# Where the residual rows, the bf16 cast of h1 and its transposing loads are issued, in a transformer layer on eight cores

## The chip, the cores and the metric

The kernel runs on all 8 cores of one Trainium2 chip. The time is in device microseconds (us), from launch to end, of the slowest of the eight cores; smaller is better. The cores do not talk to each other. Each computes 2,048 rows of the output (half of one of four batch entries) and recomputes the keys and values that it needs.

## The reference, cut to what matters

```python
# x: (4, 4096, 2048) f32; 16 heads of 128; feed-forward width I = 5632
def layer(x):
    q, k, v = heads(tokens(x) @ Wqkv.T)
    ctx = softmax(q @ k.T / sqrt(128)) @ v
    h1 = layernorm(x + ctx @ Wproj.T + bproj)
    w_gu, w_down = dequant_fp4(gate_up), dequant_fp4(down)
    gate, up = split(h1 @ w_gu.T)
    y = (silu(gate) * up) @ w_down.T
    y = y / sqrt(mean(y * y) + 1e-6)
    return layernorm(h1 + y)
```

## The kernel before, in words

Each engine has its own program, written by hand, and runs it in order; engines meet at counting semaphores. TensorE first projects keys, values and queries for the first pair of heads. Then come eight slots of attention (SLOTS), each of 128 steps (STEPS). A step is a score block, its exponential on ScalarE (`act_exp`, tiles P, three buffers), and the context matmuls. While ScalarE works, TensorE fills in matmuls of the next slot's projections. In the last slot the filling is the output projection: 16 tiles of 128 rows (TILES), each of four groups of 512 columns, 16 matmuls a group, in two PSUM banks in turn. It starts at step 60 of the last slot (OC_FIRST), so that part of it runs beside the attention's last exponentials and the rest, about eleven tiles, runs alone. This rest is called the tail below.

For one tile t of the output projection the engines work like this:

- SyncE loads the context transposed (`sp_ctx_load`, a ring of four) and the residual rows of x (`sp_xr_load`, two buffers xr). The load for tile t+2 waits until VectorE has read all of tile t (oc_evac).
- GpSimd adds the bias to the residual rows (`pool_bias`, L918).
- VectorE adds the rows to the PSUM bank group by group (L674) and takes statistics (L677, L681).
- GpSimd forms the reciprocal deviation (`pool_rstd_b`, L928 and L931), and VectorE writes the normalized tile h1f, two buffers (L687).
- GpSimd stores h1f, then does `pool_bias` for tile t+2, and only then `pool_rstd_b` for tile t+1. Its loop is this:

```python
    for tile in range(TILES):
        pool_rstd_b(g, S, M, tile)
        g.wait_ge(S.h1_done, tile + 1)
        g.dma_start(out=M.d_h1[...], in_=M.h1f[tile % 2][:])
        if tile + 2 < TILES:
            pool_bias(g, S, M, tile + 2)
```

- ScalarE casts h1f to bf16 in another order of columns (`act_h1_cast`, L505) and stores it (L509). Casts of tiles 0 to 3 stand between exponentials, at steps fixed in `act_program`; tiles 4 to 15 come after the last exponential.
- VectorE starts on the next tile only when its biased rows are there (xrb_done) and h1f of the tile before is written.

The feed-forward part follows, in four chunks of 512 rows (FCH). A chunk has 44 gate/up operations of 32 matmuls each (`pe_gate_up`, L389 and L393) and then the down projection (`pe_down`, L412). The gate/up weights are in a ring of four buffers of 1 MB (`sp_wgu_load`, L1126); SyncE issues the load for operation n+4 when operation n is done. The rows of h1 come in by transposing loads from the bf16 copy in DRAM (`sp_h1t_load`, L1118), one for each 128 rows, four for a chunk, into one of two buffers. The loads for the next chunk stand on SyncE's queue at operation 10, all four in a row.

Of the kernel before, what the change touches and what calls it, by code (L numbers as in the profile page):

```python
# [24 lines left out]
SLOTS = 8  # L25
STEPS = 128
# [13 lines left out]
TILES = TOK // 128  # L40
OC_FIRST = 60
CTXT_RING = 4
WP_EARLY = (58, 60, 62)

FCH = 4
WGU_RING = 4
WD_RING = 9
PAIR_BANKS = (0, 2, 6, 4)

# [16 lines left out]
def oc_groups_done(i):  # L66

    return max(0, STEP_UNITS * (i + 1 - OC_FIRST) // GROUP_UNITS)
# [43 lines left out]
""".split()  # L112
SEVERAL = {"ctx_stored": 2, "pk_in": 2, "wt_stored": 2, "ctxt_in": CTXT_RING, "xr_in": 2, "h1b_stored": 2, "h1t_in": 2, "wgu_in": WGU_RING, "wd_in": WD_RING, "out_last": 2, "wdx_in": 2}
POOL_ONE = "bias_in wv_in wq_in w1_in".split()
# [21 lines left out]
class Mem:  # L136


    def __init__(self, nc):
# [21 lines left out]
        def at(offset, name, shape, dt):  # L161
            return nc.alloc_sbuf_tensor_at(name, shape, dt, offset=offset)
# [18 lines left out]
        self.hffnT = at(r1, "hffnT", [128, GU_OPS, 512], BF16)  # L181
        self.wd = [at(r1 + 45056 + 4096 * j, f"wd{j}", [128, 4, 512], BF16) for j in range(WD_RING)]

# [10 lines left out]
        self.y = [at(r2 + 8192 * j, f"y{j}", [128, H], F32) for j in range(4)]  # L194
        self.wgu = [at(r3 + 8192 * j, f"wgu{j}", [128, 4, 4, 256], BF16) for j in range(WGU_RING)]

# [172 lines left out]
def pe_gate_up(t, S, M, ch, op, exact):  # L369
    kc = ch * GU_OPS + op  # L370
    b = PAIR_BANKS[kc % 4]
    t.wait_ge(S.wgu_in[kc % WGU_RING], 16 * (kc // WGU_RING + 1))
    if op == 0:
# [9 lines left out]
    elif op == 3:  # L383
        t.wait_ge(S.ctx_evac, SLOTS * QBLOCKS)
        if not exact:
            t.wait_ge(S.flag_done, 1)
    w = M.wgu[kc % WGU_RING]
    for kt in range(HC):
# [9 lines left out]
def pe_down(t, S, M, ch, oc):  # L398
    for ut in range(DN_UT):
        du = (ch * 4 + oc) * DN_UT + ut  # L400
        t.wait_ge(S.wd_in[du % WD_RING], 16 * (du // WD_RING + 1))
        if oc == 0:
# [7 lines left out]
        for tt in range(4):  # L410
            for j in range(4):
                mm = t.matmul(M.bank((oc % 2) * 4 + tt),  # L412
                              M.hffnT[:, 4 * ut + j, tt * 128:(tt + 1) * 128],
                              M.wd[du % WD_RING][:, j, :],
                              start=(ut == 0 and j == 0), stop=(ut == DN_UT - 1 and j == 3))
# [4 lines left out]
def pe_down_last(t, S, M):  # L420
# [3 lines left out]
    for tt in range(4):  # L424
        for ut in range(DN_UT):
            du = first + ut
            if tt == 0 and ut < WD_RING:
                t.wait_ge(S.wd_in[du % WD_RING], 16 * (du // WD_RING + 1))
            elif tt == 0:
# [67 lines left out]
                 scale=NORM).then_inc(S.exp_done, 1)  # L497


def act_h1_cast(a, S, M, tile):  # L500

    a.wait_ge(S.h1_done, tile + 1)
    if tile >= 2:
        a.wait_ge(S.h1b_stored[tile % 2], 16 * (tile // 2))
    a.copy(out=M.h1b[tile % 2][:].rearrange("t (u j p) -> t u j p", u=4, j=4),  # L505
           in_=M.h1f[tile % 2][:].rearrange("t (u p j) -> t u j p", u=4, j=4)
           ).then_inc(S.h1b_done, 1)
    a.wait_ge(S.h1b_done, tile + 1)
    a.dma_start(out=M.d_h1b[tile * 128:(tile + 1) * 128, :],  # L509
                in_=M.h1b[tile % 2][:]).then_inc(S.h1b_stored[tile % 2], 16)  # L510


def act_silu(a, S, M, kc):
# [30 lines left out]
def act_program(a, S, M, exact):  # L544
    a.wait_ge(S.consts, 1)
    g = 0
    while g < GROUPS:
        act_proj_evac(a, S, M, g)
        g += 1
    tile = 0  # L550
    for n in range(SLOTS * STEPS):
        act_exp(a, S, M, n)
        last = n % STEPS == STEPS - 1
        while g < groups_done(n if exact and last else n - 1):
            act_proj_evac(a, S, M, g)
            g += 1
        if n >= (SLOTS - 1) * STEPS and 4 * (tile + 1) <= oc_groups_done(n % STEPS - 5):
            act_h1_cast(a, S, M, tile)
            tile += 1
    while tile < TILES:  # L560
        act_h1_cast(a, S, M, tile)
        tile += 1

    for ch in range(FCH):
        for op in range(GU_OPS):
            act_silu(a, S, M, ch * GU_OPS + op)
        for oc in range(4 if ch + 1 < FCH else 3):
            act_y_evac(a, S, M, ch, oc)
    for tt in range(4):
        act_last_norm(a, S, M, tt)  # L570
    r = TILES - 1
    a.wait_ge(S.l_norm, 12)
    a.wait_ge(S.l_done, 4)
    a.dma_start(out=M.d_out[r * 128:(r + 1) * 128, 1024:2048],
                in_=M.res[3][:, 1024:2048]).then_inc(S.out_last[1], 16)
# [525 lines left out]
                          ).then_inc(S.ctxt_in[tile % CTXT_RING], 16)  # L1101


def sp_xr_load(y, S, M, tile):
    if tile >= 2:
        y.wait_ge(S.oc_evac, 4 * (tile - 1))
    y.dma_start(out=M.xr[tile % 2][:],
                in_=M.d_xrows[tile * 128:(tile + 1) * 128, :]).then_inc(S.xr_in[tile % 2], 16)


def sp_h1t_load(y, S, M, ch, tiles):
    if ch >= 2:
        y.wait_ge(S.up_done, GU_OPS * (ch - 1))
    for j in range(2):
        y.wait_ge(S.h1b_stored[j], 32 if ch == 0 else 16 * (TILES // 2))
    for tt in tiles:
        tile = 4 * ch + tt
        y.dma_start_transpose(out=M.h1T[ch % 2][:, tt, :, :],  # L1118
                              in_=M.d_h1b[tile * 128:(tile + 1) * 128, :]
                              ).then_inc(S.h1t_in[ch % 2], 16)  # L1120


def sp_wgu_load(y, S, M, kc):
    if kc >= WGU_RING:
        y.wait_ge(S.up_done, kc - WGU_RING + 1)
    y.dma_start(out=M.wgu[kc % WGU_RING][:].rearrange("p j u o -> p (j u o)"),  # L1126
# [13 lines left out]
def sp_program(y, S, M, exact):  # L1140
    if not exact:
        y.wait_ge(S.proj_done, group_offset(7))
        sp_codes(y, S, M, 0)
        sp_codes(y, S, M, 1)
    for c in range(SLOTS * QBLOCKS - QBLOCKS):
        if exact and c % QBLOCKS == 0:
            sp_row_max(y, S, M, c // QBLOCKS)
        sp_ctx_store(y, S, M, c)
        for u in () if exact else dequant_units(c):
            sp_weights(y, S, M, u)  # L1150
    if exact:
        sp_row_max(y, S, M, SLOTS - 1)
    y.wait_ge(S.pv_done, (SLOTS - 1) * STEPS)
    sp_xr_load(y, S, M, 0)
    sp_xr_load(y, S, M, 1)
    xr = ctxt = 0
    for i in range(STEPS):
        if i % 16 == 15:
            sp_ctx_store(y, S, M, (SLOTS - 1) * QBLOCKS + i // 16)
        if i == 34:  # L1160
            y.wait_ge(S.proj_done, SLOTS * GROUPS)
            while ctxt < CTXT_RING:
                sp_ctx_load(y, S, M, ctxt)
                ctxt += 1
        if 4 * (xr + 1) <= oc_groups_done(i - 2):
            sp_xr_load(y, S, M, xr + 2)
            xr += 1
        while ctxt - CTXT_RING < xr and 32 * (ctxt // 4 + 1) <= i:
            sp_ctx_load(y, S, M, ctxt)
            ctxt += 1  # L1170
    y.wait_ge(S.pv_done, SLOTS * STEPS)
    for j in range(2):
        y.wait_ge(S.ctx_stored[j], 16 * (SLOTS * QBLOCKS // 2))
    while xr + 2 < TILES:
        if xr == TILES - 5:
            sp_wgu_load(y, S, M, 0)
            sp_wgu_load(y, S, M, 1)
        if xr >= TILES - 4:
            sp_h1t_load(y, S, M, 0, range(2 * (xr - TILES + 4), 2 * (xr - TILES + 4) + 2))
        while ctxt < TILES and ctxt - CTXT_RING <= xr:  # L1180
            sp_ctx_load(y, S, M, ctxt)
            ctxt += 1
        sp_xr_load(y, S, M, xr + 2)
        xr += 1
    sp_wgu_load(y, S, M, 2)
    sp_wgu_load(y, S, M, 3)
    for ch in range(FCH):
        for op in range(GU_OPS):
            kc = ch * GU_OPS + op + WGU_RING
            if kc < FCH * GU_OPS:  # L1190
                sp_wgu_load(y, S, M, kc)
            if op == 10 and ch + 1 < FCH:
                sp_h1t_load(y, S, M, ch + 1, range(4))
            if op == 34 and ch == 0:
                for du in range(WD_RING):
                    sp_wd_load(y, S, M, du)
            if op == 34 and ch == FCH - 1:
                y.wait_ge(S.up_done, (FCH - 1) * GU_OPS)
                for j in range(2):
                    y.dma_start(out=M.wdx[j][:],  # L1200
                                in_=M.d_wdn[3, WD_RING + j]).then_inc(S.wdx_in[j], 16)
        for k in range(4 * DN_UT):
            du = ch * 4 * DN_UT + k + WD_RING
            if du < FCH * 4 * DN_UT - 2:
                sp_wd_load(y, S, M, du)
    for tt in range(4):
        r = 4 * (FCH - 1) + tt
        cols = slice(0, 2048 if tt < 3 else 1024)
        y.wait_ge(S.l_norm, 3 * tt + (3 if tt < 3 else 2))
        if tt < 3:  # L1210
            y.wait_ge(S.l_done, tt + 1)
        y.dma_start(out=M.d_out[r * 128:(r + 1) * 128, cols],
                    in_=M.res[res_slot(r)][:, cols]).then_inc(S.out_last[0], 16)
# [140 lines left out]
```

## Time and profile before

| | us |
|---|---|
| median of 3 runs | 4144.91 (4142.04 to 4147.2) |
| profiled execution | 4153.74 |
| its span on the slowest core, core 2 | 4152.0 |
| spans of the eight cores | 4127.6 to 4152.0 |
| TensorE busy, core 2 | 4060.1 (98%) |
| ScalarE busy, core 2 | 1400.2 (34%) |
| GpSimd busy, core 2 | 286.4 (7%) |

The profile follows one execution. A span goes from a core's first to its last instruction. PE is TensorE, PEld its weight loads, DVE VectorE, ACT ScalarE, POOL GpSimd and SP SyncE; a q behind the name is the engine's issuing of DMAs. L505 is line 505 of the kernel. All times of an instruction are counted from the start of the span.

### The profile page before, as it was taken

Reading aid. Unit: us, or ns where it says so; the run is one execution under the profiler, and the core shown is the slowest. Engines: PE = TensorE matmul, PEld = TensorE weight load, DVE = VectorE, ACT = ScalarE, POOL = GpSimd, SP = SyncE. Lnnn points to the kernel's source line nnn. Section 1 sums busy time; section 2 is a strip of 40 time slices with the busy share of each in tenths; the row PEclk is TensorE's granted clock in tenths of the full one; section 3 lists DMA queues with packets and bytes.
Section 4 is the critical chain, followed back from the end, with each engine's and each line's share of the span. In section 5 each row is a group of like instructions: output and inputs, shape, how many; then the busy total and the mean of one; then the engine's idle time right before and its main releaser. Section 6 shows DMA issues by size and latency. Waiting matters only on the chain.

```text
span 4152.0 us, 66120 instructions; the slowest of 8 cores (4127.6 to 4152.0 us)
## 1 busy us (share of the span) xinstructions
PE 4060.1 (98%) x26491; PEld 2296.5 (55%) x26881; DVE 948.6 (23%) x1433; ACT 1400.2 (34%) x1610; POOL 286.4 (7%) x434
## 2 busy tenths in 40 slices
PE   7999999999999999999999999999999999999998
PEld 4666666666666766666554444444444444444443
DVE  0054452222222223220234100022100300022124
ACT  1355555555555555557642100000000000000001
POOL 1100000000000000000223000000000000000000
PEclk9999999999999999999999999999999999999999
DMA  9777776465655655656459545447444654446433
GB/s 146 130 172 169 178 165 126 107 137 121 124 119 118 140 104 120 135 119 111 110 157 261 191 167 199 159 155 231 152 157 152 201 189 152 157 164 216 162 127 123
DMA packets 251041, 635.65 MB, mean 153 GB/s; under 512 B 115184, under 2 KB 137712, under 8 KB 212720
## 3 DMA queue, kind: packets, MB, share of 16 engines
q1 hardware_dynamic: 202496, 426.29, 31.6%
q0 software_dynamic: 45792, 196.10, 25.5%
q10 hardware_dynamic: 2448, 8.91, 0.5%
q8 instruction: 225, 3.69, 0.4%
q14 instruction: 80, 0.66, 0.0%
HBM read 643.83 MB, written 119.54 MB: 184 GB/s over the span
## 4 chain that ended last, share of the span: by engine, by line
PE 93%; SPq 2%; DMA 2%; issue 1%; ACT 1%; DVE 0%; POOL 0%; ACTq 0%; DVEq 0%; POOLq 0%
PE pJ L283 16%; PE pC L339 11%; PE pJ L269 11%; PE pS L320 10%; PE pS L412 7%; PE pS L393 7%; PE pS L389 7%; PE pC L389 4%; PE pJ L393 3%; PE pC L393 3%; PE pJ L389 3%; PE pJ L361 3%; PE pC L412 3%; PE pJ L412 3%; SPq L1118 2%
## 5 line engine op out<-in xcount | busy, mean ns | idle before, releaser
L496 ACT ACTIVATE P<-pS 128x1024 bf16<-128x1024 f32 x1024 | 1027.8, 1026 | 356.8 <-PE pS L320 342.6
L283 PE MATMUL pJ<-x,wq 128*128 128x512 bf16 x2984 | 756.9, 381 | 28.5 <-DMA x<-xc 23.8
L339 PEld LDWEIGHTS pC<-V,P 128*128 128x128 bf16 x8192 | 549.8, 98 | 168.0 <-issue 11.3
L339 PE MATMUL pC<-V,P 128*128 128x129 bf16 x8192 | 634.0, 220 | 3.6 <-DVE ctxg L613 3.1
L320 PE MATMUL pS<-Q,K 128*128 128x512 bf16 x1829 | 561.7, 379 | 18.9 <-ACT P L496 7.5
L269 PE MATMUL pJ<-wq,x 128*128 128x256 bf16 x4096 | 514.8, 273 | 0.4
L283 PEld LDWEIGHTS pJ<-x,wq 128*128 128x128 bf16 x3072 | 301.0, 98 | 381.9 <-issue 33.4
L269 PEld LDWEIGHTS pJ<-wq,x 128*128 128x128 bf16 x4096 | 400.7, 98 | 134.8
L609 DVE RECIPROCAL rcp<-pC 128x4 f32<-128x4 f32 x64 | 11.7, 183 | 1477.9 <-PE pC L339 1477.9
L393 PE MATMUL pS<-h1T,wgu 128*128 128x512 bf16 x1408 | 318.3, 379 | 0.0
L389 PE MATMUL pS<-h1T,wgu 128*128 128x512 bf16 x1408 | 318.3, 379 | 0.0
L412 PE MATMUL pS<-wd,hffnT 128*128 128x512 bf16 x1380 | 303.1, 379 | 1.5
L905 POOL DMA_DIRECT2D x<-xc x256 | 138.3, 558 | 1743.6 <-PE pJ L283 1089.0
L361 PE MATMUL pJ<-wp,ctxT 128*128 128x512 bf16 x1001 | 232.8, 380 | 9.1 <-DVE r L674 7.8
L517 ACT ACTIVATE sg<-pS 128x512 bf16<-128x512 f32 x88 | 52.4, 597 | 532.5 <-PE pS L389 532.5
L389 PEld LDWEIGHTS pS<-h1T,wgu 128*128 128x128 bf16 x1408 | 137.9, 98 | 166.0
L412 PEld LDWEIGHTS pS<-wd,hffnT 128*128 128x128 bf16 x1408 | 137.8, 98 | 166.1
L393 PEld LDWEIGHTS pS<-h1T,wgu 128*128 128x128 bf16 x1408 | 137.8, 98 | 166.1
L389 PE MATMUL pC<-h1T,wgu 128*128 128x512 bf16 x704 | 163.5, 386 | 13.5 <-DMA wgu<-wgu_scr 13.5
L695 DVE TENSOR_TENSOR hffnT<-sg,pS 128x512 bf16<-128x512 bf16 x88 | 60.6, 688 | 498.6 <-PE pS L393 492.1
L361 PEld LDWEIGHTS pJ<-wp,ctxT 128*128 128x128 bf16 x1024 | 100.0, 98 | 129.7 <-issue 11.4
L320 PEld LDWEIGHTS pS<-Q,K 128*128 128x128 bf16 x2048 | 157.0, 98 | 11.5 <-issue 8.4
(107 smaller groups left out, 2647.8 us busy)
## 6 DMA issues: line engine op xcount, KB each, us to landing
wgu<-wgu_scr SPq DMA_DIRECT2D x176, 1024.0 KB, 4.9
x<-xc POOLq DMA_DIRECT2D x256, 512.0 KB, 12.4
wd<-wdn_scr SPq DMA_DIRECT2D x174, 512.0 KB, 3.5
wgu_scr<-bits SPq DMA_DIRECT2D x44, 1024.0 KB, 5.1
wdn_scr<-bits SPq DMA_DIRECT2D x44, 512.0 KB, 4.6
xr<-xrows SPq DMA_DIRECT2D x16, 1024.0 KB, 7.1
h_scr<-h1f POOLq DMA_DIRECT2D x16, 1024.0 KB, 7.1
res<-h_scr POOLq DMA_DIRECT2D x16, 1024.0 KB, 8.9
```

Of the source, the lines that this page charges most:

```text
L269: mm = t.matmul(out[:, tt * 256:(tt + 1) * 256], x[:, hc, (2 * h + tt) * 128:(2 * h + tt + 1) * 128], M.wq[:, pair, 1, hc, :], start=(hc = ...
L283: mm = t.matmul(out, M.wq[:, pair, part, hc, h * 128:(h + 1) * 128], x[:, hc, :], start=(hc == 0), stop=(hc == HC - 1))
L320: mm = t.matmul(M.pS[n % 2][:, h * 512:(h + 1) * 512], M.K[s % 2][:, l, kt * 128:(kt + 1) * 128], M.Q[s % 2][:, l, qc * 512:(qc + 1) * 512 ...
L339: mm = t.matmul(M.pC[:, o:o + 129], M.P[n % 3][:, h * 512 + qt * 128:h * 512 + (qt + 1) * 128], M.V[s % 2][:, 2 * p + h, l, :], start=(p = ...
L361: mm = t.matmul(M.bank(6 + q % 2), M.ctxT[tile % CTXT_RING][:, hc, :], M.wp[2 * oc + hc // 8][:, hc % 8, :], start=(hc == 0), stop=(hc == ...
L389: mm = t.matmul(M.bank(b), w[:, kt % 4, kt // 4, 0:128], M.h1T[ch % 2][:, :, kt, :], start=(kt == 0), stop=(kt == HC - 1))
L393: mm = t.matmul(M.bank(b + 1), w[:, kt % 4, kt // 4, 128:256], M.h1T[ch % 2][:, :, kt, :], start=(kt == 0), stop=(kt == HC - 1))
L412: mm = t.matmul(M.bank((oc % 2) * 4 + tt), M.hffnT[:, 4 * ut + j, tt * 128:(tt + 1) * 128], M.wd[du % WD_RING][:, j, :], start=(ut == 0 an ...
L496: a.activation(out=M.P[n % 3][:], in_=M.pS[n % 2][:], func=AF.Exp, bias=0.0, scale=NORM).then_inc(S.exp_done, 1)
L695: v.tensor_tensor(out=M.hffnT[:, kc % GU_OPS, :], in0=M.sg[kc % 2][:], in1=M.bank(PAIR_BANKS[kc % 4] + 1), op=ALU.mult).then_inc(S.h_done, 1)
L905: g.dma_start(out=M.x[gc % 2][:, 4 * q:4 * q + 4, :], in_=M.d_x[w, ch, :, 4 * q:4 * q + 4, :]).then_inc(S.x_in[(gc % 2) * 4 + q], 16)
L1118: y.dma_start_transpose(out=M.h1T[ch % 2][:, tt, :, :], in_=M.d_h1b[tile * 128:(tile + 1) * 128, :]).then_inc(S.h1t_in[ch % 2], 16)
```

## The change

Three things are done to the code. First, the cast of a tile is cut into four casts of 512 columns; beside the exponentials one such quarter follows each of four exponentials. Second, the residual rows of tiles 2 to 15 are no longer loaded by SyncE: ScalarE issues the load for tile t+2 behind the store of the bf16 copy of tile t. Third, the transposing loads for the next chunk are issued one at a time, at operations 8, 15, 22 and 29. The transposing loads for the first chunk stay in pairs.

```diff
+H1T_OPS = (8, 15, 22, 29)
-def act_h1_cast(a, S, M, tile):
+def act_h1_cast(a, S, M, k):
+    tile, ut = divmod(k, 4)
+    cols = slice(512 * ut, 512 * (ut + 1))
     a.wait_ge(S.h1_done, tile + 1)
     if tile >= 2:
         a.wait_ge(S.h1b_stored[tile % 2], 16 * (tile // 2))
-    a.copy(out=M.h1b[tile % 2][:].rearrange("t (u j p) -> t u j p", u=4, j=4),
-           in_=M.h1f[tile % 2][:].rearrange("t (u p j) -> t u j p", u=4, j=4)
-           ).then_inc(S.h1b_done, 1)
+    cast = a.copy(out=M.h1b[tile % 2][:, cols].rearrange("t (j p) -> t j p", j=4),
+                  in_=M.h1f[tile % 2][:, cols].rearrange("t (p j) -> t j p", j=4))
+    if ut < 3:
+        return
+    cast.then_inc(S.h1b_done, 1)
     a.wait_ge(S.h1b_done, tile + 1)
     a.dma_start(out=M.d_h1b[tile * 128:(tile + 1) * 128, :],
                 in_=M.h1b[tile % 2][:]).then_inc(S.h1b_stored[tile % 2], 16)
+    if tile + 2 < TILES:
+        a.wait_ge(S.oc_evac, 4 * (tile + 1))
+        a.dma_start(out=M.xr[tile % 2][:], in_=M.d_xrows[(tile + 2) * 128:(tile + 3) * 128, :]
+                    ).then_inc(S.xr_in[tile % 2], 16)
...
-        if n >= (SLOTS - 1) * STEPS and 4 * (tile + 1) <= oc_groups_done(n % STEPS - 5):
-            act_h1_cast(a, S, M, tile)
-            tile += 1
-    while tile < TILES:
-        act_h1_cast(a, S, M, tile)
-        tile += 1
+        if n >= (SLOTS - 1) * STEPS and 4 * (k // 4 + 1) <= oc_groups_done(n % STEPS - 5):
+            act_h1_cast(a, S, M, k)
+            k += 1
+    for k in range(k, 4 * TILES):
+        act_h1_cast(a, S, M, k)
...
-def sp_xr_load(y, S, M, tile):
-    if tile >= 2:
-        y.wait_ge(S.oc_evac, 4 * (tile - 1))
-    y.dma_start(out=M.xr[tile % 2][:],
-                in_=M.d_xrows[tile * 128:(tile + 1) * 128, :]).then_inc(S.xr_in[tile % 2], 16)
...
-        if 4 * (xr + 1) <= oc_groups_done(i - 2):
-            sp_xr_load(y, S, M, xr + 2)
-            xr += 1
+        if 4 * (done + 1) <= oc_groups_done(i - 2):
+            done += 1
...
-    while xr + 2 < TILES:
-        if xr == TILES - 5:
+    for tile in range(done, TILES - 2):
+        if tile == TILES - 5:
             sp_wgu_load(y, S, M, 0)
             sp_wgu_load(y, S, M, 1)
...
-        sp_xr_load(y, S, M, xr + 2)
-        xr += 1
...
-            if op == 10 and ch + 1 < FCH:
-                sp_h1t_load(y, S, M, ch + 1, range(4))
+            if op in H1T_OPS and ch + 1 < FCH:
+                tt = H1T_OPS.index(op)
+                sp_h1t_load(y, S, M, ch + 1, range(tt, tt + 1))
```

## Rows read from the trace of the kernel before

**Rows 1.** Spans and mean granted TensorE clock, two of eight cores.

```profile
core 2: 4152.0 us, clock 0.996
...
core 5: 4136.4 us, clock 0.997
```

**Rows 2.** TensorE's waits, core 2: instruction, releaser, total us, times, longest.

```profile
PE pC L389 <- DMA wgu<-wgu_scr: 13.5, 2, 7.1
PE pJ L361 <- DVE r L674: 7.8, 3, 3.3
```

**Rows 3.** The same waits of core 5.

```profile
PE pJ L361 <- DVE r L674: 3.4, 1, 3.4
...
PE pC L389 <- DMA wgu<-wgu_scr: 2.8, 1, 2.8
```

**Rows 4.** TensorE's waits, core 2, from 2020 to 2140 us.

```profile
PE pS L320 <- ACT P L496: 6.0, 4, 1.9
```

**Rows 5.** Timeline around tile 0's cast, core 2: start, us, engine, operation, [idle before].

```profile
2015.26 1.02 ACT L496 ACTIVATE P<-pS 128x1024 bf16<-128x1024 f32 x1 [0.94 <-PE pS L320]
...
2018.44 0.59 PE L320 MATMUL pS<-Q,K 128*128 128x512 bf16 x2
...
2029.93 3.94 ACT L505 CAST h1b<-h1f 128x2048 bf16<-128x2048 f32 x1
...
2033.95 0.38 ACTq L509 DMA_DIRECT2D h1b_scr<-h1b  x1
...
2035.66 0.59 PE L320 MATMUL pS<-Q,K 128*128 128x512 bf16 x2 [1.34 <-ACT P L496]
```

**Rows 6.** ScalarE's groups by shape, core 2: busy, mean ns | idle before.

```profile
L505 ACT CAST h1b<-h1f 128x2048 bf16<-128x2048 f32 x16 | 62.6, 3915 | 123.0 <-DVE h1f L687 123.0
...
L528 ACT COPY y<-pS 128x512 f32<-128x512 f32 x32 | 18.8, 586 | 298.9 <-PE pS L412 298.9
```

**Rows 7.** Timeline of the tail's end, core 2: tile 15's rows, tile 14's h1f.

```profile
2269.55 0.52 SPq L1107 DMA_DIRECT2D xr<-xrows  x1
...
2279.23 4.50 POOL L918 TENSOR_TENSOR xr<-xr,bias 128x2048 f32<-128x2048 f32 x1 [9.94 <-DMA xr<-xrows]
2283.71 0.22 POOL L928 TENSOR_SCALAR epsB<-aggB 128x1 f32<-128x1 f32 x1
...
2284.75 1.34 DVE L687 TENSOR_SCALAR h1f<-r,aggB,rstdB 128x2048 f32<-128x2048 f32 x1 [5.87 <-POOL rstdB L931]
2286.24 3.85 ACT L505 CAST h1b<-h1f 128x2048 bf16<-128x2048 f32 x1 [14.08 <-DVE h1f L687]
```

**Rows 8.** Timeline, core 2: h1f of tile 4, ahead of the tail.

```profile
2134.09 1.35 DVE L687 TENSOR_SCALAR h1f<-r,aggB,rstdB 128x2048 f32<-128x2048 f32 x1 [1.33 <-POOL rstdB L931]
```

**Rows 9.** Residual-row loads L1107, core 2, from 2150 to 2275 us.

```profile
L1107 SPq DMA_DIRECT2D xr<-xrows x9: 504/525/1951, 2151.7 to 2269.5; - x9
...
DMA to landing us min/median/max: 6.4/7.8/9.7
```

**Rows 10.** The same loads from 2020 to 2140 us.

```profile
L1107 SPq DMA_DIRECT2D xr<-xrows x5: 352/353/357, 2024.7 to 2131.7; - x5
...
DMA to landing us min/median/max: 5.2/5.4/5.4
```

**Rows 11.** Transposing loads L1118, core 2: issue time ns, minimum, median, maximum.

```profile
L1118 SPq DMA_TRANSPOSE h1T<-h1b_scr x16: 2968/4513/9328, 2241.3 to 3311.6; - x16
```

**Rows 12.** The chain that ended last, core 2: start, us, what.

```profile
2850.53 11.26 DMA wgu<-wgu_scr
```

**Rows 13.** Timeline, core 2, around the loads for chunks 2 and 3.

```profile
2827.96 22.47 SPq L1118 DMA_TRANSPOSE h1T<-h1b_scr  x4
...
2862.06 5.93 PE L389 MATMUL pC<-h1T,wgu 128*128 128x512 bf16 x16 [7.07 <-DMA wgu<-wgu_scr]
...
2867.83 3.62 PE L393 MATMUL pC<-h1T,wgu 128*128 128x512 bf16 x16
...
3326.85 5.65 PE L389 MATMUL pC<-h1T,wgu 128*128 128x512 bf16 x16 [6.47 <-DMA wgu<-wgu_scr]
```

More of the change, by code:

```diff
@@ L549, in act_program @@
         g += 1
-    tile = 0
+    k = 0
     for n in range(SLOTS * STEPS):
@@ L1153, in sp_program @@
     y.wait_ge(S.pv_done, (SLOTS - 1) * STEPS)
-    sp_xr_load(y, S, M, 0)
-    sp_xr_load(y, S, M, 1)
-    xr = ctxt = 0
+    for tile in range(2):
+        y.dma_start(out=M.xr[tile][:],
+                    in_=M.d_xrows[tile * 128:(tile + 1) * 128, :]).then_inc(S.xr_in[tile], 16)
+    done = ctxt = 0
     for i in range(STEPS):
@@ L1164, in sp_program @@
                 ctxt += 1
-        if 4 * (xr + 1) <= oc_groups_done(i - 2):
-            sp_xr_load(y, S, M, xr + 2)
-            xr += 1
-        while ctxt - CTXT_RING < xr and 32 * (ctxt // 4 + 1) <= i:
+        if 4 * (done + 1) <= oc_groups_done(i - 2):
+            done += 1
+        while ctxt - CTXT_RING < done and 32 * (ctxt // 4 + 1) <= i:
             sp_ctx_load(y, S, M, ctxt)
@@ L1173, in sp_program @@
         y.wait_ge(S.ctx_stored[j], 16 * (SLOTS * QBLOCKS // 2))
-    while xr + 2 < TILES:
-        if xr == TILES - 5:
+    for tile in range(done, TILES - 2):
+        if tile == TILES - 5:
             sp_wgu_load(y, S, M, 0)
             sp_wgu_load(y, S, M, 1)
-        if xr >= TILES - 4:
-            sp_h1t_load(y, S, M, 0, range(2 * (xr - TILES + 4), 2 * (xr - TILES + 4) + 2))
-        while ctxt < TILES and ctxt - CTXT_RING <= xr:
+        if tile >= TILES - 4:
+            tt = 2 * (tile - TILES + 4)
+            sp_h1t_load(y, S, M, 0, range(tt, tt + 2))
+        while ctxt < TILES and ctxt - CTXT_RING <= tile:
             sp_ctx_load(y, S, M, ctxt)
             ctxt += 1
-        sp_xr_load(y, S, M, xr + 2)
-        xr += 1
     sp_wgu_load(y, S, M, 2)
```

## The prediction

> **What bounds the kernel now.** I read the spans of the cores first: core 2 has 4152.0 us, core 5 has 4136.4, both at a granted clock of nearly 1 [rows 1]. So this is the fast level of 2.4 GHz nearly throughout, and the clock is no cause of the difference. TensorE is busy 98% of the span, so only what makes TensorE wait counts. Its list of waits shows three causes that the change touches. On core 2 they are 13.5 us for gate/up weights, 7.8 us for VectorE's reading of the output projection's banks [rows 2], and 6.0 us, in four waits, for exponentials between 2020 and 2140 us [rows 4]. On core 5 the first two are 2.8 and 3.4 us [rows 3]. A perfect repair of all three would be worth some 27 us on core 2 and 12 on core 5, before what the clock adds.
>
> **The quarter casts.** One cast takes 3.9 us [rows 6]. At tile 0 it follows an exponential, holds the next ones back, and the score matmul waits 1.34 us [rows 5]. Four such casts lie beside exponentials and there are four waits, 6.0 us in all [rows 4]. A copy of 512 columns takes 0.586 us [rows 6] and an exponential of 1024 takes 1.02 [rows 5]. If both cost the same per column, the fixed part of an instruction is 0.15 us (an estimate). A quarter then costs (3.915 - 0.15)/4 + 0.15 = 1.09 us and four cost 4.37. The lower bound is 3.91 in all, with no fixed part; the upper is 4.7, if the fixed part is 0.25. I take 4.37.
>
> Beside the exponentials a step lasts 0.94 + 1.02 = 1.96 us of ScalarE's time [rows 5]. A quarter and an exponential need 2.11, so ScalarE falls behind by 0.15 in each of four steps, and by two DMA issues of 0.38 [rows 5] and 0.35 [rows 10] and some 0.2 of waits. That is about 1.5 us. How much can it fall behind? An exponential ends at 2016.28 and the score matmuls that need its buffer start at 2018.44 [rows 5]: 2.16 us. The quarters fit, and 6.0 us are gained. If they do not fit, the gain is between 0 and 6.
>
> **The residual rows.** This part decides the result. SyncE now issues the load for tile t+2 when VectorE has read tile t. In the changed kernel the load is behind the cast and the store of tile t on ScalarE, and the cast cannot start before h1f of tile t is written. GpSimd, in turn, adds the bias for tile t+2 *before* it computes the reciprocal deviation of tile t+1, without which h1f of tile t+1 cannot be written. The second half of this is visible already: for tile 15 the bias starts at 2279.23, 9.68 us after its load was issued, and the deviation of tile 14 starts at 2283.71, when the bias ends [rows 7]. New is that the load itself waits for h1f. So there is a closed loop with one tile in it, from h1f of tile t to h1f of tile t+1:
>
> - h1f's end to the cast's start, 0.15 (2286.09 to 2286.24) [rows 7]
> - four quarter casts, 4.37
> - the gap to the store, 0.08, and its issue, 0.38 [rows 5], and 0.05 to the next issue (estimated)
> - the landing of 1 MB of rows, L
> - 0.15 from landing to GpSimd's start (estimated)
> - the bias, 4.50, and from the start of L928 to the end of h1f 2284.75 + 1.34 - 2283.71 = 2.38 [rows 7]
>
> The sum is 12.06 + L. For L the tail's nine loads show 6.4 to 9.7 us, median 7.8 [rows 9]; the five beside attention show 5.2 to 5.4 [rows 10]. In the new order the store of the bf16 tile, 512 KB, is just ahead of the load on the same queue, while the slower pace thins the traffic. I take 7.9, near the tail's median, and keep 5.4 and 9.7 as ends. A link of the loop is then 20.0 us, with 17.5 and 21.8 as ends.
>
> Now from h1f of tile 4, which ends at 2135.44 [rows 8], to h1f of tile 14, which ends at 2286.09 [rows 7], there are ten links. They take 150.65 us, 15.1 each, the stalls included. The loop needs more than that even with its shortest landing, so it sets the pace of all ten, up to the load for tile 15. TensorE can't run away, since it has two banks and VectorE reads the next tile only when h1f is written. The first load meets little traffic (6.4), so ten links take 18.5 + 9 x 20.0 = 198.5 us. The tail gets 47.9 us longer. The ends are +24.0 (L = 5.4, ten times 17.46) and +67 (L = 9.7). The tail stalls of 7.8 us lie inside the 150.65 and are not subtracted again. On core 5 the links were shorter by the difference of the waits, 7.8 - 3.4, so it loses 52.3.
>
> Beside the exponentials the same loop costs nothing. Five load issues lie between 2024.7 and 2131.7, 26.8 us apart [rows 10]. Four quarters in four steps take 3 x 1.96 + 1.09 = 7.0 us instead of 4.37, and with L = 5.4 the loop needs about 20 us. Some 6 us of cover remain. SyncE loses the row loads, and its weight and transposing loads come no later.
>
> The Trainium skill speaks against this move (DMA: Bandwidth & Descriptors, "Issuing engines are not separate DMA queues"): DMAs started by ScalarE, SyncE or GpSimd run on the same 16 DMA engines and interleave. By that rule another issuing engine shortens no landing, and no run here yet shows it.
>
> **The transposing loads.** SyncE spends 22.47 us on issuing four [rows 13]. The weight load behind them then needs 11.26 us [rows 12]. TensorE waits 7.07 and, for the next chunk, 6.47 us [rows 13]. After each wait 16 matmuls take 5.93 and 5.65 us where others take 3.62 [rows 13]; the granted clock has fallen for a moment to the lower level, 1.2 GHz, and this adds 2.3 + 2.0. Core 2 has 13.5 + 4.3 = 17.8 us to gain, core 5 has 2.8 + 2.2 = 5.0.
>
> One load at a time occupies SyncE for 4.5 us, 9.3 at most [rows 11]. A weight load is issued three operations before its use, 6 x 3.5 = 21 us. Even the worst pair, 9.3 + 11.26 = 20.6, just fits, and the usual one easily. I take the whole 17.8. The lower bound is nothing, if the single ones stall TensorE as well.
>
> **The sum**, against the profiled execution's 4153.7 us: 4153.7 + 47.9 - 6.0 - 17.8 = 4177.8 for core 2. Core 5 gives 4136.4 + 1.7 around the span + 52.3 - 6.0 - 5.0 = 4179.4. Cores that stalled differently before come out alike, since the same loop paces them. The profiled execution is 8.8 us above the median of the runs, 4144.9, mostly because of core 2's two weight stalls; with these gone I expect no such difference and forecast 4178 for the median, 33 us or 0.8% slower.
>
> **Rivals.**
>
> *The rows land as fast as beside attention.* With L = 5.4 the tail loses only 24.0, and the gains of 23.8 cancel it: 4153.9. For it speaks that the five loads with little traffic took 5.4 [rows 10]; against it, that none of nine in the tail was under 6.4 [rows 9]. With core 5's numbers it is 4155.5, so it ends at the border of no change. Chance 0.08.
> The Trainium skill's fit (DMA: Bandwidth & Descriptors, "Anatomy of one DMA") is 2.0 us + bytes/436 GB/s, an estimate of 4.4 us for 1 MB, which would give a link of 16.5 and about 4144, no change; the trace disagrees, its fastest such load taking 5.2.
>
> *The loop does not close, or is shorter than the tail's present pace: faster.* The row loads would have to leave the path, so that the casts' 6.0 and the weights' 17.8 remain, and also the 7.8 stall goes: core 2 would be at 4122, the slowest core near 4128. The point from which the kernel is faster at all is L = 3.7 us (a link of 15.7). Against it: the code orders cast, store and load on one engine, and no landing is under 5.2. Chance 0.05.
>
> *Single transposing loads still stall TensorE.* One slow issue with a slow landing eats the 21 us of cover. The price is 17.8 at most: 4195. Against it is the first batch of four, for chunk 1, which caused none of the two waits. Chance 0.05.
>
> *The quarters still delay exponentials* as the whole cast does: +6, so 4184. The slack of 2.16 against 1.5 speaks against it. Chance 0.07.
>
> **How the numbers follow.** My forecast has 0.75. The range 4155 to 4195 goes from L = 5.5 to L = 9.5 and takes in both of the last rivals. A measurement of this kernel tells about 0.2% (8.3 us) from no change. Faster: 0.05. Same, which is the first rival's better half: 0.06. Slower: 0.89.
>
> **What would show it.** In the changed profile: a new, large wait of TensorE at L361 for VectorE (r L674), about 5 us in each of ten tiles; h1f (L687) every 20 us in the tail; GpSimd's bias (L918) ending just as L928 starts; quarter casts of 1.1 us; no wait of L320 for exponentials near the casts; no wait of L389 for weights. I am wrong if h1f comes every 14 to 15 us in the tail.

## The result, and the profile after

The changed kernel takes 4181.05 us (median of 4 runs, 4179.87 to 4182.23), the kernel before 4144.91 (median of 3). The ratio is 1.0088, 95% interval 1.0068 to 1.0107: slower by 0.9%, 36 us. The forecast was 4178. Medians and ratios here and below leave out executions in which the clock of a die was disturbed; where only one or two are left, they are given singly. The ratios are the recorded ones and can differ a little from the quotient of the two medians.

The spans of all eight cores are close together now, 4164.8 to 4178.3 where they were 4127.6 to 4152.0, as the forecast had it from one common pace. Two of them, with the mean granted clock:

```profile
core 2: 4164.8 us, clock 0.995
...
core 5: 4178.3 us, clock 0.994
```

TensorE's waits on core 5, the slowest (instruction, releaser, total us, times, longest), answer to [rows 2 to 4]:

```profile
PE pJ L362 <- DVE r L683: 47.3, 10, 21.1
...
PE pS L321 <- ACT P L497: 1.3, 3, 0.9
```

The wait for VectorE at the output projection has gone from 3.4 to 47.3 us on this core and is on every tile of the tail. The waits for gate/up weights are gone from the list, on all eight cores. The waits for exponentials have fallen from 7.0 to 1.3 us.

ScalarE's groups by shape, core 5, against [rows 6]: a quarter takes 1.11 us.

```profile
L509 ACT CAST h1b<-h1f 128x512 bf16<-128x512 f32 x64 | 67.6, 1111 | 171.6 <-DVE h1f L696 171.6
```

One turn of the loop in the timeline of core 5, from h1f of one tile to h1f of the next. It answers to [rows 7].

```profile
2163.95 1.35 DVE L696 TENSOR_SCALAR h1f<-r,aggB,rstdB 128x2048 f32<-128x2048 f32 x1 [6.84 <-POOL rstdB L940]
2165.44 4.14 ACT L509 CAST h1b<-h1f 128x512 bf16<-128x512 f32 x4 [14.06 <-DVE h1f L696]
...
2166.30 15.66 PE L362 MATMUL pJ<-wp,ctxT 128*128 128x512 bf16 x64 [4.26 <-DVE r L683]
...
2169.65 0.34 ACTq L515 DMA_DIRECT2D h1b_scr<-h1b  x1
2170.08 0.40 ACTq L519 DMA_DIRECT2D xr<-xrows  x1
...
2176.68 4.50 POOL L927 TENSOR_TENSOR xr<-xr,bias 128x2048 f32<-128x2048 f32 x1 [10.20 <-DMA xr<-xrows]
2181.16 0.22 POOL L937 TENSOR_SCALAR epsB<-aggB 128x1 f32<-128x1 f32 x1
...
2182.20 1.35 DVE L696 TENSOR_SCALAR h1f<-r,aggB,rstdB 128x2048 f32<-128x2048 f32 x1 [5.18 <-POOL rstdB L940]
```

Read it from above. Everything in it waits for the line before: the casts for h1f, the row load for the casts and the store, the bias for the load (GpSimd idle 10.20 us), the deviation (L937) for the bias, h1f for the deviation. One turn is 2182.20 - 2163.95 = 18.25 us. TensorE works 15.66 us of it, at the lower clock for part of that, and then waits for VectorE. It does not set the pace: the statistics of this tile are ready at 2177.02 us, the bias ends at 2181.18.

There is one turn unlike the others. The same timeline later, tile 11 to tile 12:

```profile
2252.45 19.39 SPq L1120 DMA_TRANSPOSE h1T<-h1b_scr  x4
...
2256.86 1.35 DVE L696 TENSOR_SCALAR h1f<-r,aggB,rstdB 128x2048 f32<-128x2048 f32 x1 [7.15 <-POOL rstdB L940]
...
2262.99 0.47 ACTq L519 DMA_DIRECT2D xr<-xrows  x1
...
2288.08 4.48 POOL L927 TENSOR_TENSOR xr<-xr,bias 128x2048 f32<-128x2048 f32 x1 [28.69 <-DMA xr<-xrows]
...
2293.59 1.35 DVE L696 TENSOR_SCALAR h1f<-r,aggB,rstdB 128x2048 f32<-128x2048 f32 x1 [23.66 <-POOL rstdB L940]
```

This row load, for tile 13, is issued at 2262.99, in the middle of four transposing loads for the first chunk, and needs 25 us to land. The turn takes 36.7 us. SyncE no longer stops for row loads, so the two pairs of transposing loads go out as one group of four. Before, on the same core, the four also followed each other closely, but the row load for tile 13 stood ahead of them on SyncE's own queue and that for tile 14 between the pairs:

```profile
2238.61 0.51 SPq L1107 DMA_DIRECT2D xr<-xrows  x1
2239.28 12.52 SPq L1118 DMA_TRANSPOSE h1T<-h1b_scr  x2
2251.92 0.49 SPq L1107 DMA_DIRECT2D xr<-xrows  x1
2252.57 17.11 SPq L1118 DMA_TRANSPOSE h1T<-h1b_scr  x2
```

No row load of that tail took more than 9.0 us to land. So no gap between the transposing loads was lost. What changed is where the row load starts: no longer in line with them on SyncE's queue but on another, in the middle of the group. All ten row loads of the tail on this core (start and issue time of the instruction in ns; landing in us), against [rows 9], which are of core 2:

```profile
L519 ACTq DMA_DIRECT2D xr<-xrows x10: 395/396/468, 2133.3 to 2317.2; - x10
...
DMA to landing us min/median/max: 5.6/6.4/24.9
```

Every core has such a turn, between the casts of tiles 11 and 12: 22.4 us on core 2, 24.7 on core 0, 30.2 on core 6.

### The profile page after: what moved, and what is told of

Same layout as the page of the kernel before. It is cut to its first block, busy times and chain, and to the rows that moved or that the text cites. A ratio compares the mean times of both kernels' runs of the same rounds, so it can differ in the third digit from the quotient of the medians.

```text
span 4178.3 us, 66672 instructions; the slowest of 8 cores (4164.8 to 4178.3 us)
## 1 busy us (share of the span) xinstructions
PE 4087.4 (98%) x26881; PEld 2297.5 (55%) x26881; DVE 947.9 (23%) x1433; ACT 1404.7 (34%) x1658; POOL 286.1 (7%) x434
## 4 chain that ended last, share of the span: by engine, by line
PE 92%; DMA 3%; issue 1%; ACT 1%; POOL 1%; DVE 1%; ACTq 0%; POOLq 0%; DVEq 0%
PE pJ L284 15%; PE pC L340 11%; PE pJ L270 10%; PE pS L321 10%; PE pS L394 7%; PE pS L413 7%; PE pS L390 7%; PE pJ L390 4%; PE pC L394 4%; PE pC L390 4%; PE pJ L394 4%; PE pJ L413 3%; PE pC L413 3%; DMA xr<-xrows 2%; PE pJ L362 2%
## 5 line engine op out<-in xcount | busy, mean ns | idle before, releaser
L321 PE MATMUL pS<-Q,K 128*128 128x512 bf16 x2048 | 609.0, 379 | 1.3 <-ACT P L497 1.3
L390 PE MATMUL pS<-h1T,wgu 128*128 128x512 bf16 x1408 | 318.2, 379 | 0.0
L362 PE MATMUL pJ<-wp,ctxT 128*128 128x512 bf16 x1024 | 245.9, 393 | 47.3 <-DVE r L683 47.3
L390 PEld LDWEIGHTS pS<-h1T,wgu 128*128 128x128 bf16 x1408 | 137.8, 98 | 166.2
L390 PE MATMUL pJ<-h1T,wgu 128*128 128x512 bf16 x704 | 159.1, 379 | 0.0
```

The lines of the kernel that those rows point to most:

```text
L321: mm = t.matmul(M.pS[n % 2][:, h * 512:(h + 1) * 512], M.K[s % 2][:, l, kt * 128:(kt + 1) * 128], M.Q[s % 2][:, l, qc * 512:(qc + 1) * 512 ...
L362: mm = t.matmul(M.bank(6 + q % 2), M.ctxT[tile % CTXT_RING][:, hc, :], M.wp[2 * oc + hc // 8][:, hc % 8, :], start=(hc == 0), stop=(hc == ...
L390: mm = t.matmul(M.bank(b), w[:, kt % 4, kt // 4, 0:128], M.h1T[ch % 2][:, :, kt, :], start=(kt == 0), stop=(kt == HC - 1))
```

## The experiments

Each was profiled and timed beside the kernel before; "before" after a time is the kernel before on the same chip. The line numbers move a little from kernel to kernel.

### Rows back on SyncE, the rest as changed

```diff
 (changed kernel)
-    if tile + 2 < TILES:                       # ScalarE, end of act_h1_cast
-        a.wait_ge(S.oc_evac, 4 * (tile + 1))
-        a.dma_start(out=M.xr[tile % 2][:], ...)
...
+            sp_xr_load(y, S, M, done + 2)       # SyncE, beside attention
...
+        sp_xr_load(y, S, M, tile + 2)           # SyncE, tail, behind sp_ctx_load
```

> The changed kernel with the residual-row loads back on SyncE, where the kernel before has them; quarter casts and single transposing loads stay. Theory (the rows' place behind the cast closes the loop and costs all of the loss): the links between casts in the tail go from 18.3 back to about 15 us, and the gains of the other two parts stay, 6 us of casts and on the slowest core some 10 us of weight waits: about 4130 us (4124 to 4138), ratio to before about 0.996. Rival (the quarter casts or the single transposing loads carry part of the loss): above 4146.

Measured: 4131.7 us (median of 4), before 4151.1; ratio 0.9957 (0.9937 to 0.9976). In the profiled execution all cores lie between 4121.0 and 4129.8. The waits of its slowest core, core 5:

```profile
PE pJ L362 <- DVE r L679: 4.0, 1, 4.0
...
PE pS L321 <- ACT P L497: 1.1, 2, 0.9
```

On this core the ten links from tile 4's cast to tile 14's take 147.1 us, 14.7 each, where the changed kernel's core 5 needs 201.7. One part, the place of the row loads, carries the whole loss, about 50 us between this kernel and the changed one. The rival is out. The other two parts together make the kernel 0.4% faster.

### Only the rows moved

```diff
 (kernel before; act_h1_cast(tile) with the whole cast)
     a.dma_start(out=M.d_h1b[...], in_=M.h1b[tile % 2][:])...
+    if tile + 2 < TILES:
+        a.wait_ge(S.oc_evac, 4 * (tile + 1))
+        a.dma_start(out=M.xr[tile % 2][:], ...)
...
 (SyncE)
-        sp_xr_load(y, S, M, xr + 2)
```

> The kernel before with only the residual rows moved to ScalarE, behind the store of the whole cast; whole casts and four transposing loads in a row as before. Theory: the links are 0.25 us shorter than in the changed kernel, since a whole cast takes 3.9 and not 4.2 us, so about 18.0; the 6 us of exponentials' waits and the weight waits of 3 to 13 us are back: about 4190 us (4183 to 4200). Rival (the cuts into quarters make the chain long): near 4150.

Measured: 4197.8 and 4209.2 us, before 4151.1. The loop needs no quarters to close. The times are 8 and 19 us over the 4190 that was expected. A part of that is in TensorE's waits for exponentials, 8.9 to 10.1 us on the eight cores, where the kernel before has 6.9 to 7.5; the rest I did not trace. On the slowest core, core 7, row loads land in 5.7 to 12.8 us, median 7.2:

```profile
L516 ACTq DMA_DIRECT2D xr<-xrows x10: 396/624/1558, 2147.5 to 2321.1; - x10
...
DMA to landing us min/median/max: 5.7/7.2/12.8
```

### The bias behind the deviation

```diff
 (changed kernel, GpSimd)
     for tile in range(TILES):
         pool_rstd_b(g, S, M, tile)
+        if 1 <= tile < TILES - 1:
+            pool_bias(g, S, M, tile + 1)
         g.wait_ge(S.h1_done, tile + 1)
...
-        if tile + 2 < TILES:
-            pool_bias(g, S, M, tile + 2)
```

> The changed kernel with GpSimd's bias for tile t+2 behind the reciprocal deviation of tile t+1 instead of ahead of it. The row loads stay behind the cast. This takes the second half of the loop away. Theory: h1f of a tile no longer waits for rows; what is left is that the bias of 4.5 us lies between two tiles on VectorE's way, which gives links of about 15.6 us (0.7 + two groups of 3.45 + 0.7 + statistics 1.6 + deviation 0.95 + bias 4.5): 27 us less over ten links and some of the one late landing hidden too, about 4150 us (4142 to 4158). Rival (ScalarE's queue delivers the rows too slowly whatever GpSimd's order): links stay at 18, above 4170.

Measured: 4172.0 and 4178.7 us. Most of the 27 us did not come. The casts of core 0 start at 2152.56, 2173.95, 2186.67 and 2208.05: links of 21.4 and 12.7 us in turn, 17.1 on average, where 15.6 were expected; one late link takes 27.3. The wait for rows is gone from the turns of 12.7; a new term is in those of 21.4. The timeline of core 3:

```profile
2170.08 4.50 POOL L927 TENSOR_TENSOR xr<-xr,bias 128x2048 f32<-128x2048 f32 x1
2170.21 5.46 DVE L696 TENSOR_SCALAR h1f<-r,aggB,rstdB 128x2048 f32<-128x2048 f32 x1 [1.33 <-POOL rstdB L940]
2175.81 4.16 ACT L509 CAST h1b<-h1f 128x512 bf16<-128x512 f32 x4 [18.89 <-DVE h1f L696]
```

VectorE's h1f takes 5.46 us instead of 1.35 when the bias starts 0.13 us ahead of it. It ends 1.09 us after the bias: the two hardly ran side by side. The same slow h1f comes up beside attention: on core 3 TensorE waits 5.4 us for exponentials between 2000 and 2140 us, where the changed kernel has no such wait. My sum had neither term, so this kernel shows that GpSimd's order matters and doesn't give the loop a clean price.

The Trainium skill (SBUF — State Buffer, "SBUF: two separate sides") says that the port pair which VectorE and GpSimd share is held by one of them for a whole instruction while the other waits, on VectorE's side for instructions in a two-port mode or with two inputs in SBUF. The trace agrees with the waiting, with 5.46 us for 1.35; in which mode this instruction runs, no run here shows.

### The row load ahead of the casts

```diff
 (changed kernel, act_h1_cast)
     cols = slice(512 * ut, 512 * (ut + 1))
+    if ut == 0 and tile + 2 < TILES:
+        a.wait_ge(S.oc_evac, 4 * (tile + 1))
+        a.dma_start(out=M.xr[tile % 2][:], ...)
     a.wait_ge(S.h1_done, tile + 1)
...
-    if tile + 2 < TILES:
-        a.wait_ge(S.oc_evac, 4 * (tile + 1))
-        a.dma_start(out=M.xr[tile % 2][:], ...)
```

> The changed kernel with the row load for tile t+2 still on ScalarE's queue but ahead of the wait for h1f and the four casts of tile t, as soon as VectorE has read tile t. This takes the first half of the loop away. Theory: the load is issued some 8 us earlier, links fall to about 14 to 15 us, the gains of the other two parts stay: about 4130 us (4122 to 4138). Rival (a row load on ScalarE's queue lands late behind the bf16 stores, or costs exponentials): above 4146.

Measured: 4160.9 us (one execution), before 4151.1: 20 us better than the changed kernel, and some 30 worse than expected. The profile of this kernel is not of this execution, so the links of 37 to 45 us that the expectation of "Both" below quotes from it show only where to look.

### The first chunk's transposing loads one at a time

```diff
 (changed kernel, SyncE, tail)
-        if tile >= TILES - 4:
-            tt = 2 * (tile - TILES + 4)
-            sp_h1t_load(y, S, M, 0, range(tt, tt + 2))
         while ctxt < TILES and ctxt - CTXT_RING <= tile:
             ...
+        if TILES - 9 <= tile < TILES - 5:
+            tt = tile - TILES + 9
+            sp_h1t_load(y, S, M, 0, range(tt, tt + 1))
```

> The changed kernel with one more edit: the four transposing loads for the first chunk, which in its profile go out in a row beside the row load for tile 14, are issued one at a time, behind the context loads of tiles 7 to 10. Theory: the loop stays (links of 18.3 us), and only the one long link goes, 37 us on the slowest core and 22 to 30 on the others: about 4172 us (4164 to 4178). Rival (the row load for tile 14 is late for another reason, or four single collisions cost as much): 4180 as the changed kernel.

Measured: 4171.4 us (median of 4; 4169.9 to 4172.6), ratio 1.0052 (1.0033 to 1.0071). So the meeting with the group of four costs the changed kernel some 10 us by the times, which do not overlap (the intervals of the two ratios just do), and the closed loop the rest: 4171.4 here against 4131.7 with the rows back on SyncE, 40 us. (The late load is that for tile 13; the expectation has 14 by a miscount.) The landings of the slowest core, core 6, and its wait:

```profile
DMA to landing us min/median/max: 5.4/6.7/14.1
```

```profile
PE pJ L362 <- DVE r L683: 38.0, 10, 11.9
```

The longest landing on a slowest core fell from 24.9 to 14.1 us and did not go back to the median.

### Only the quarters, and only the single loads

The first is the kernel before with the part of the diff in `act_h1_cast` and `act_program` that cuts the cast; the second is the kernel before with `H1T_OPS`.

> The kernel before with only the casts cut into quarters. Theory: the four waits of 1.3 to 1.9 us for exponentials go and nothing else changes, 6 us faster, about 4140 us, ratio 0.9986. Rival (quarters hold the exponentials up or lengthen the tail): 4146 or more.

> The kernel before with only the next chunks' transposing loads issued one at a time. Theory: no TensorE wait for gate/up weights is left at L389; the slowest core gains its waits and the slow matmuls after them, some 5 to 18 us: about 4137 us (4132 to 4142). Rival (single loads stall as well): 4146 with waits for weights.

Quarters only: 4150.2 us (median of 8; 4139.8 to 4155.1), before 4147.0, ratio 0.9997 (0.9978 to 1.0016). The expected 6 us are not in the time, though they are in the trace. The waits of core 7 and core 4 of one execution:

```profile
PE pC L390 <- DMA wgu<-wgu_scr: 4.8, 2, 2.4
...
PE pJ L362 <- DVE r L679: 1.6, 1, 1.6
PE pS L321 <- ACT P L497: 1.1, 2, 0.9
```

```profile
PE pJ L362 <- DVE r L679: 17.7, 3, 12.9
PE pC L390 <- DMA wgu<-wgu_scr: 7.1, 2, 3.7
...
PE pS L321 <- ACT P L497: 1.1, 2, 0.9
```

On every core the wait for exponentials fell (to 1.1, on two cores to 1.5 us). But on three of eight cores the wait at the output projection rose to 16.7 to 19.8 us, where the kernel before has 2.2 to 8.0, and the slowest core makes the time. On core 4 the timeline shows where it comes from: SyncE needs 22.02 us to issue a pair of transposing loads, and the row load behind it is late.

```profile
2248.59 22.02 SPq L1123 DMA_TRANSPOSE h1T<-h1b_scr  x2
...
2270.73 0.52 SPq L1112 DMA_DIRECT2D xr<-xrows  x1
...
2285.25 4.48 POOL L923 TENSOR_TENSOR xr<-xr,bias 128x2048 f32<-128x2048 f32 x1 [19.57 <-DMA xr<-xrows]
```

The quarters alone do not cause it by any edge in the code that I can name; whether they shift the meeting of the transfers or this is scatter, these runs don't say.

Single loads only: 4135.1 and 4136.2 us, before 4147.0, some 11 us faster. No core waits at L390; the slowest core has 4133.3 us. This is what was expected. The first experiment has the quarters on top of this, and 4131.7 us; the difference of some 4 us agrees with the casts' 6, but two executions cannot show it.

### Both: rows ahead and transposing loads spread

The two edits above together.

> The row load ahead of h1f's wait on ScalarE's queue together with the first chunk's transposing loads issued one at a time behind the context loads of tiles 7 to 10. With the row loads ahead alone, one link lasted 37 to 45 us, while the four transposing loads were in flight, and the fastest run took 4160.9. Theory (the loop is open and only that meeting of transfers held it up): links of 14 to 15 us throughout, about 4127 us (4119 to 4134). Rival (rows on ScalarE's queue are slow by themselves): above 4146.

Measured: 4175.9 and 4182.2 us. A miss, and the one that taught most. The row loads of core 4, and two transposing loads of its timeline:

```profile
L508 ACTq DMA_DIRECT2D xr<-xrows x9: 346/346/367, 2144.5 to 2300.5; - x9
...
DMA to landing us min/median/max: 8.6/17.9/31.8
```

```profile
2193.10 20.75 SPq L1108 DMA_TRANSPOSE ctxT<-ctx_scr  x1
2201.76 0.35 ACTq L508 DMA_DIRECT2D xr<-xrows  x1
2214.00 12.73 SPq L1120 DMA_TRANSPOSE h1T<-h1b_scr  x1
2219.30 4.48 POOL L927 TENSOR_TENSOR xr<-xr,bias 128x2048 f32<-128x2048 f32 x1 [25.31 <-DMA xr<-xrows]
```

The loop is open here: the load goes out without waiting for its tile's h1f. Yet the median landing is 17.9 us, and other cores have landings of up to 49.2. Issuing this transposing load of the context takes 20.75 us, and a later one on this core 32.56, where those of the kernel before took 1.33 to 6.24 us on core 2; that of h1 takes 12.73, where 4.5 was the median [rows 11]. Row loads and transposing loads now start at the same point of a tile, on two queues, and both are slow. In the changed kernel the delay behind the casts kept them apart in most turns. Spreading h1's loads gained 10 us with the row loads behind the casts; with the row loads ahead of them it cost 15 to 21, against the one execution of 4160.9.

### Rows first, and rows apart

Two kernels to tell a slow queue from a bad moment. In one all loads are on SyncE, the row load ahead of the transposing loads of its turn. In the other the rows stay on ScalarE's queue, ahead of the casts, and SyncE waits for their landing.

```diff
 (rows back on SyncE, tail)
+        sp_xr_load(y, S, M, tile + 2)
         if tile >= TILES - 4:
             tt = 2 * (tile - TILES + 4)
             sp_h1t_load(y, S, M, 0, range(tt, tt + 2))
         while ctxt < TILES and ctxt - CTXT_RING <= tile:
             sp_ctx_load(y, S, M, ctxt)
             ctxt += 1
-        sp_xr_load(y, S, M, tile + 2)
```

```diff
 (row load ahead of the casts; SyncE, tail)
+        y.wait_ge(S.xr_in[tile % 2], 16 * (tile // 2 + 2))
         if tile >= TILES - 4:
             tt = 2 * (tile - TILES + 4)
             sp_h1t_load(y, S, M, 0, range(tt, tt + 2))
```

> Quarter casts and single transposing loads as changed; the residual rows on SyncE, but in the tail ahead of the transposing load of each turn (context, and h1's pairs), not behind it. Beside attention, where a row load goes out half a microsecond ahead of a context load on this queue, it lands in 5.4 us. Theory (a row load is late when transposing loads are ahead of it or beside it): landings of 5.5 to 7 us in the tail, TensorE's waits there fall from 3.4 to 4.9 us to under 2, about 4128 us (4121 to 4133). Rival (the transposing loads started right behind slow the rows as much): 4132 or more, waits of 4 us and over.

> The kernel with the row load on ScalarE's queue ahead of h1f's wait, and with one wait more on SyncE: in the tail it issues the transposing loads of a turn only when the row load of that turn has landed. The two kinds of transfer no longer start together on two queues. Theory (the loop is open, and landings of 25 to 45 us came from a row load and a transposing load in flight at the same time on two queues): landings of 5 to 7 us, links of 13.8 to 14.5 us, about 4128 us (4121 to 4136). Rival (ScalarE's queue is slow for rows, or the held-back context loads come late): above 4146.

Rows first: 4146.4 us (median of 10), before 4151.7, ratio 0.9987 (0.9975 to 1.0000), a miss. In the profiled execution five cores have 4117.4 to 4125.6 us. Their rows land as expected (core 1):

```profile
L1112 SPq DMA_DIRECT2D xr<-xrows x9: 328/332/337, 2142.3 to 2253.2; - x9
DMA to landing us min/median/max: 5.0/5.9/8.8
```

The other three have 4136.6 to 4142.4 and one link of 22 to 33 us each late in the tail, where the pairs for h1 are. So on five cores context loads right behind a row load did no harm, and the long links of the other three lie where the pairs of h1 loads are.

Rows apart: 4128.5 to 4163.7 us in five executions, median 4141.7, ratio 0.9961 (0.9936 to 0.9986). In the profiled execution six of eight cores have 4118.0 to 4123.1. On core 0 the rows land like this, from ScalarE's queue:

```profile
L508 ACTq DMA_DIRECT2D xr<-xrows x9: 346/346/347, 2142.5 to 2253.4; - x9
DMA to landing us min/median/max: 4.9/5.9/10.7
```

A median of 5.9 against 17.9: ScalarE's queue delivers rows as fast as SyncE's when the transposing loads wait for them, and TensorE has no wait at the output projection on this core. So the rows can stay on ScalarE's queue without the loop. This gives the loop no price of its own, since two edits set the kernel apart from the changed one, the place ahead of the casts and SyncE's wait. What remains is core 6 with 4161.9 us. It waited 10.6 us at the output projection, 4.7 of them for a context load, and 22.7 at the first gate/up operation, not for weights but for the transposed rows of h1:

```profile
PE pS L390 <- DMA h1T<-h1b_scr: 22.7, 1, 22.7
...
PE pJ L362 <- DMA ctxT<-ctx_scr: 4.7, 1, 4.7
```

```profile
L1120 SPq DMA_TRANSPOSE h1T<-h1b_scr x4: 7215/10366/29344, 2261.7 to 2312.1; - x4
```

The four transposing loads of h1 took 7.2 to 29.3 us each to issue there, where those of core 0 took 1.8 to 5.1, and the last began at 2312.1. SyncE had waited 27.4 us for two row loads before them. This is near the expectation's rival that held-back loads come late, on one core of eight and mostly with h1's loads; why single ones take so long to issue stays open.

### In turn

```diff
 (rows first)
         sp_xr_load(y, S, M, tile + 2)
-        if tile >= TILES - 4:
-            tt = 2 * (tile - TILES + 4)
-            sp_h1t_load(y, S, M, 0, range(tt, tt + 2))
+        y.wait_ge(S.xr_in[tile % 2], 16 * (tile // 2 + 2))
+        if tile >= TILES - 6:
+            tt = tile - TILES + 6
+            sp_h1t_load(y, S, M, 0, range(tt, tt + 1))
```

> Quarter casts and single transposing loads as changed, and in the tail one kind of transfer at a time, all on SyncE: the row load of a turn first, a wait until it has landed, then one transposing load of h1 (at tiles 10 to 13, one each) and the context load. Theory (what is left of TensorE's waits in the tail comes from rows in flight beside transposing loads, above all pairs of them): no landing of rows over 10 us, no wait at the output projection over 2 us on any core, all cores between 4116 and 4128, about 4127 us for the slowest (4120 to 4133). Rival (the transposing loads for h1 collide with the stores of h1f and the bf16 tile, or come too late for the first gate/up operation): waits at the first gate/up operation, or single links over 20 us, 4135 or more.

Measured: 4133.7 us (median of 7; 4130.7 to 4136.2), before 4157.2; ratio 0.9946 (0.9926 to 0.9967). The time is as expected, the reason only in part. Waits at the output projection are 2.8 to 7.6 us, not under 2, and each core still has a row landing of 13 to 16 us. On the slowest, core 1:

```profile
DMA to landing us min/median/max: 4.9/6.2/15.7
```

Against the first experiment's 0.9957 the intervals overlap. Both beat the kernel before and the changed one.

## Why the prediction was right

**The loop** was right in every edge, and the sum came out within 0.1%; that it came so close is luck, as the next paragraph shows. For core 5 it said 4179.4 and the profiled span with 1.7 around it is 4180.0. Its tail took, from tile 4's cast to tile 14's, 2330.36 - 2128.65 = 201.7 us, before 2284.27 - 2136.39 = 147.9: +53.8 where 52.3 were forecast.

**Two terms inside it were off and cancelled on this core.** The landing L was put at 7.9 us; the median is 6.4. Nine turns add up to 165.0 us, 18.3 each, where 178.5 were forecast. The four quarters take 4.14 back to back, not 4.37, and the rest of the constant, 12.06 - 4.37 = 7.7, came out as 18.25 - 4.14 - 6.4 = 7.7. The other error is the tenth turn, 36.7 us, which I had not seen coming: I looked at what SyncE loses with the row loads and called it no cost, when their place on its queue had kept every row load in line with the transposing loads. On core 5 it took 16.7 us more than the forecast turn, and the nine others gave 13.5 back. On core 2, where it is 22.4 us, the tail has 189.7, and the span is 4164.8. So "4177.8 for core 2" was 11 us too high. TensorE's waits, forecast at about 5 us in each of ten tiles, are 26.2 us in nine of them, 2.9 each, and 21.1 in the tenth.

**The casts** cost 5.7 us less waiting on core 5, against 6.0. The exponentials catch up, as worked out. **The weights' waits** are gone. The runs with single loads alone give 11 us of the time; the 17.8 was a figure for one core of one execution.

**The rivals.** The rows landing as fast as beside attention is out (6.4 against 5.4, and a late one). That another issuing engine shortens no landing was weighed with the rule of the Trainium skill (DMA: Bandwidth & Descriptors, "Issuing engines are not separate DMA queues") that they all run on the same 16 DMA engines; medians of 5.9 us from either queue agree. The fit that stands with the first rival is given by the Trainium skill (DMA: Bandwidth & Descriptors, "Anatomy of one DMA") for the GpSimd path, and these loads are on other queues. The rival of single transposing loads that still stall TensorE, at 0.05, was about transfers in each other's way, as what was missed is, but in another place. In the rival of a shorter loop one figure is wrong: L = 3.7 us is where core 5 would equal its own span before, and against the median of 4144.9 the prediction's numbers give about 4.4. No run came near either.

**Open** are the single cores that stay long in executions of "rows apart", "rows first" and "quarters only", and why a row load beside transposing loads needs 14 to 49 us sometimes and 7 at other times.

## What to carry to other kernels

Before a load is moved to another engine's queue, follow in program order what that engine waits for ahead of it, and from the load's data back to that same wait. If the way closes, the new period is the sum round the loop, and it can be added up from the trace before anything is built. Look also at what the old place ordered: on one queue the row load stood ahead of the transposing loads or between them, and here row loads that started together with transposing loads of another queue landed three times as late in the median (17.9 us against 5.9), and the one that started in the middle of the group of four took 24.9.

## What the runs showed of the hardware

- A row load of 1 MB landed in 5.9 us in the median, from SyncE's queue ("rows first", core 1) or ScalarE's ("rows apart", core 0), when it started ahead of the transposing loads. Started with transposing loads on the other queue ("both", core 4) it took 17.9 us in the median and 31.8 at most, and issuing one transposing load of the context took up to 32.56 us, where those of the kernel before took at most 6.24 on core 2.
- VectorE's normalization of 128x2048 took 5.46 us instead of 1.35 when GpSimd's addition of 128x2048 began 0.13 us ahead of it.
- In the tail of the changed kernel TensorE ran at the lower level for a part of most turns, but not after each stall: on core 5 the 64 matmuls of a tile took 15.53 to 16.14 us in six tiles, after stalls of 2.19 to 21.08 us, and 13.97 in three, after stalls of 0.30, 2.44 and 1.26. The mean granted clock was 0.89 from 2150 to 2340 us and 1.00 from 2400 to 2600. In the turns of the loop this cost nothing, since h1f waited for the bias and not for TensorE:

```profile
2150.00:2340.00 190.00, 142.98 (x602) 60.93 (x601) 64.97 (x93) 38.67 (x38) 53.29 (x36) 0.89 0.67 180
2400.00:2600.00 200.00, 200.00 (x928) 90.64 (x927) 19.96 (x29) 17.34 (x29) 0.00 (x0) 1.00 0.51 176
```

The columns are the stretch, its length, the busy time of TensorE, its weight loads, VectorE, ScalarE and GpSimd, the granted clock, the DMA share and GB/s.
